# Retention, queries and keys of batches 1 to 3 worked inside the attention of the batch before, through one PSUM bank

## The reference, cut to what matters

```python
sq, sk, sv = (_lin(x, Wsq, bsq), _lin(x, Wsk, bsk), _lin(x, Wsv, bsv))   # 16 heads of 8
g = jnp.exp(-jax.nn.softplus(_lin(x, Wg, bg)))                          # one gate a head
def step(M, inp):                                                       # over the 1024 tokens
    g_t, k_t, v_t, q_t = inp
    M = g_t[..., None, None] * M + k_t[..., None] * v_t[..., None, :]
    h = jnp.einsum('bhd,bhde->bhe', q_t, M)
    return (M, h)
Q, K = _l2norm(_lin(Hseq, Wq, bq)), _l2norm(_lin(Hseq, Wk, bk)); V = _lin(x, Wv, bv)
scores = jnp.einsum('bhqd,bhkd->bhqk', Q, K) * jax.nn.softplus(temp)
out = jnp.einsum('bhqk,bhkd->bhqd', jax.nn.softmax(scores, axis=-1), V)
return _lin(out, Wo, bo)
```

## Time and profile before

| | |
|---|---|
| median of 3 runs | 1385.3 us (1382.85 to 1386.9) |
| the profiled execution | 1391.36 us, of which its span 1389.4 us |
| PE busy | 1071.3 us, 77% of the span |
| ACT busy | 975.3 us, 70% |
| DVE busy | 742.7 us, 53% |
| POOL busy | 325.7 us, 23% |
| constants, up to the first DMA of the first layer norm | 0 to 4.75 us of the span |
| retention, all batches | 504.6 to 669.6 us |
| queries and keys, all batches | 669.6 to 735.1 us |
| attention | 735.1 to 1220.0 us |

### The profile page before, as it was taken

The page is one execution under the profiler, slowest core; times in us unless marked ns, Lnnn a source line. Parts: engine busy times, 40 slices in busy tenths (PEclk is TensorE's granted clock), DMA queues, the critical chain, the costliest instruction groups (busy, mean ns, idle before and its releaser), DMA issues. The chain is left out here.

```text
span 1389.4 us, 17492 instructions
## 1 busy us (share of the span) xinstructions
PE 1071.3 (77%) x5850; PEld 393.9 (28%) x5850; DVE 742.7 (53%) x1012; ACT 975.3 (70%) x884; POOL 325.7 (23%) x194
## 2 busy tenths in 40 slices
PE   4748777777799956777446888888888888679996
PEld 3213333333344422332341111111111111134443
DVE  5869998987566648998481001200300300256664
ACT  3767665754688832221336999999999999658885
POOL 3117776766111114665100000000000000011110
PEclk8769999999899978998777999999999999879998
DMA  2000100100100000000001111111111111000002
GB/s 73 0 16 30 31 30 30 60 30 31 32 30 30 31 24 0 0 0 1 8 0 33 24 24 32 37 24 28 22 33 34 24 24 28 11 31 31 30 30 61
DMA packets 24188, 36.48 MB, mean 26 GB/s; under 512 B 7362, under 2 KB 11970, under 8 KB 24130
## 3 DMA queue, kind: packets, MB, share of 16 engines
q1 hardware_dynamic: 24130, 35.71, 9.5%
HBM read 16.82 MB, written 6.29 MB: 17 GB/s over the span
## 5 line engine op out<-in xcount | busy, mean ns | idle before, releaser
L1674 ACT ACTIVATE att_prob<-att_s_ps 128x1536 f32<-128x1536 f32 x342 | 459.2, 1912 | 7.4 <-PE att_s_ps L1588 7.3
L1603 PE MATMUL att_o_ps<-att_prob,att_va 128*32 128x512 f32 x2048 | 273.9, 607 | 0.5 <-ACT att_prob L1674 0.5
L1705 DVE COPY att_o_sb<-att_o_ps 128x512 f32<-128x512 f32 x32 | 22.1, 691 | 381.7 <-PE att_o_ps L1603 381.7
L1588 PE MATMUL att_s_ps<-att_q_st,att_k_st 32*128 32x512 f16 x1024 | 134.4, 388 | 80.8 <-ACT att_prob L1674 76.1
L685 POOL TENSOR_TENSOR scan_hc<-scan_state,scan_c_rep 128x1024 f32<-128x1024 f32 x64 | 151.9, 2392 | 71.9 <-DVE scan_state L642 71.7
L787 POOL TENSOR_TENSOR ffn_veps<-ffn_mv,all_eps 128x4 f32<-128x4 f32 x16 | 9.1, 570 | 575.3 <-DVE ffn_mv L944 575.3
L642 DVE TENSOR_TENSOR_SCAN scan_state<-scan_decay,scan_drive_ps 128x1024 f32<-128x1024 f32 x64 | 142.9, 2270 | 0.3 <-ACT scan_decay L615 0.3
L282 PE MATMUL scan_y_ps<-scan_hc,all_ident 128*128 128x512 f32 x256 | 130.2, 634 | 8.3 <-DVE scan_y_sb L661 6.2
L1588 PEld LDWEIGHTS att_s_ps<-att_q_st,att_k_st 32*128 32x128 f16 x1024 | 33.1, 91 | 327.2 <-ACT att_prob L1674 315.9
L619 ACT ACTIVATE scan_c_rep<-scan_c_ps 128x1024 f32<-128x1024 f32 x64 | 65.4, 1022 | 80.4 <-PE scan_c_ps L282 80.1
L1012 DVE SCALAR_TENSOR_TENSOR ffn_hid_lo<-ffn_hid,ffn_share,ffn_hid_hi 128x1024 f16<-128x1024 f32 x64 | 81.9, 1283 | 48.8 <-ACT ffn_hid_hi L920 48.1
(11 more groups left out here) (215 smaller groups left out, 1505.8 us busy)
## 6 DMA issues: line engine op xcount, KB each, us to landing
...
att_q_st<-hv_part SPq DMA_DIRECT2D x64, 64.0 KB, 2.1
att_k_st<-hv_part SPq DMA_DIRECT2D x64, 64.0 KB, 2.1
...
```

The lines of the kernel that those rows point to most:

```text
L1588: last = pe.matmul(s_ps[e % 2][:, n, :], k_st[rows, g % 2, kc * P:(kc + 1) * P], q_st[rows, g % 2, HALVES[half]], start=True, stop=True)
L1603: last = pe.matmul(o_ps[half][32 * j:32 * j + 32, :], va[:, g % 2, kc, j, :], prob[:, (GH * v + j) % RING, :], start=kc == 0, stop=kc == K ...
L1674: act.activation(prob[:, first % RING:first % RING + n, :], s_ps[e % 2][:, 0:n, :], ACT.Exp).then_inc(exped.sem, 1)
```

## The change

Retention and queries-and-keys run as stages of their own for batch 0 only. For batches 1 to 3 the same results are made by pieces of work, called guests here, that all engines do between their attention instructions of the batch before, at step `u = v % 64`. All guest products go through one PSUM bank of 512 columns, `b_ps`, in halves of 512 tokens. To free that bank, the two score buffers become a triple and a pair, so that Exp instructions take 1536 and 1024 columns in turn. The guest gate is Exp on ACT (table of Exp stays loaded), then +1 and a reciprocal on DVE. Copies that ACT did (splits, keys, queries, values, h) go to DVE, squares to POOL; the root stays on ACT. Guest products write `kv_sb` in SBUF instead of multiplying in PSUM, so the guest scan reads gate and input from SBUF. SP's `stack` of a batch's first head group waits for the last of the guest's splits. `v_tok` and `part` hold two batches in turn.

Besides: the retention weights, `wo`, softplus(temp), the output bias and `a_neg` are loaded or worked out in `load_constants`; the staging copies `dt_b` and `h_b` are gone; all `Fori` loops outside the first layer norm and the store are written out; at the end of each stage POOL clears the stage's semaphores; the splitting of the expert weights in `selective_scan` takes every seventh step; `divide` is spread over steps 5, 7, 9, 11 and the projection is at steps 12 and 14 (before: all at step 5, and 11 and 13).

The diff, cut to its core:

```diff
 def load_constants(t, whole):
+                sp.dma_start(w_all[:, 0:len(RET_MATS), :], d["ret_mats"]).then_inc(ret_loaded, 16)
+                sp.dma_start(w_all[:, len(RET_MATS):W, :], d["wsv"]).then_inc(ret_loaded, 16)
+                ... (head_sum, att_mats, bqk, wo: four more DMAs; SP waits for all)
+                act.activation(t.ret_hi[:, :, :], w_all[:, :, :], ACT.Copy, scale=WS).then_inc(ret_high, 1)
+                dve.scalar_tensor_tensor(t.ret_lo[:, :, :], w_all[:, :, :], WS, t.ret_hi[:, :, :], ALU.mult,
+                                         ALU.subtract)
 def attention(t):
-    WIDE, BEHIND, RING = (2, 3, 12) if following else (3, 2, 15)
+    WIDE, CYCLE, BEHIND, RING = (3, 2), 5, 2, 15
-    DIVIDE_AT, PROJECT_AT = W + 5, (W + 11, W + 13)
+    DIVIDE_AT, PROJECT_AT = (5, 7, 9, 11), (12, 14)
+    TURN_X_AT, NORMAL_AT, TURN_Z_AT = (0, 6), (2, 8), (4, 10)
+    MAKE_AT = 11
+    OPEN_AT, INVERT_AT = (16, 19), ((17, 18), (22, 25))
+    SUM_AT = (34, 45)
+    PROJECT_QK_AT = (37, 40, 47, 48)
+    REDUCE_AT = (39, 42, 49, 50)
+    ROOT_AT, RECIPROCAL_AT, UNIT_AT, TURN_QK_AT = 53, 54, (55, 55, 56, 56), (56, 57, 58, 59)
+    def closes(e):
+        return (tiles_of(e)[-1] + 1) // GH > tiles_of(e)[0] // GH
+    def unit_at(u):
+        return [w for w in range(UNITS) if 20 + 3 * w // 2 == u]
 # PE, after scores(e) and the values that are due, where a group closes step v:
+                def make(n, p):
+                    elif x == 2:
+                        pe.wait_ge(gated.sem, gated.at(n - 1, h))
+                        last = parts(b_ps[:, :], t.ret_hi[:, w, :], t.ret_lo[:, w, :], z_hi[:, HALVES[h]], z_lo[:, HALVES[h]])
+                def key_value(n, w):
+                        pe.wait_ge(kv_done.sem, kv_done.at(n - 1, w - 1))
+                    parts(b_ps[:, :], t.ret_hi[:, i, :], t.ret_lo[:, i, :], z_hi[:, HALVES[h]],
+                          z_lo[:, HALVES[h]]).then_inc(v_made.sem, 1)
+                def add_heads(n, h):
+                    for odd in range(2):
+                        for c in range(4):
+                            last = pe.matmul(b_ps[32 * c:32 * c + 32, :], t.head_sum[:, odd, :], qm[:, 4 * odd + c, :],
+                                             start=not odd, stop=bool(odd))
 # ACT
+                def gate(n, h):
+                    act.wait_ge(made.sem, made.at(n - 1, 4 * h + 1))
+                    act.activation(g_sb[:, HALVES[h]], b_ps[:, :], ACT.Exp, bias=t.col("bg"),
+                                   scale=1.0 / WS).then_inc(gated.sem, 1)
+                def root(n):
+                    act.wait_ge(clipped.sem, clipped.at(n - 1))
+                    act.activation(rn[:, :, :], ss[:, :, :], ACT.Sqrt).then_inc(rooted.sem, 1)
                 for e in range(GROUPS):
                     ... (the Exp of group e)
+                    if closes(e):
+                        n, u = guest(first // GH)
+                        if u in (MAKE_AT + 2, MAKE_AT + 6):
+                            gate(n, (u - MAKE_AT) // 4)
+                        if u == ROOT_AT:
+                            root(n)
 # DVE
+                def invert_gate(n, h, k):
+                    dve.reciprocal(g_sb[:, cols], g_sb[:, cols]).then_inc(gate_made.sem, 1)      # 256 columns
+                def outer(n, w):
+                    dve.scalar_tensor_tensor(kv_sb[:, w % 2, :], b_ps[:, :], t.bsv_large[:, m:m + 1], k_sb[:, HALVES[h]],
+                                             ALU.add, ALU.mult).then_inc(kv_done.sem, 1)
+                def scan(n, w):
+                    dve.tensor_tensor_scan(mem[:, m, :], g_sb[:, HALVES[h]], kv_sb[:, w % 2, :],
+                                           mem[:, m, HALF - 1:HALF] if h else 0.0, ALU.mult,
+                                           ALU.add).then_inc(scanned.sem, 1)
 # POOL
+                def weigh(n, w):
+                    pool.tensor_tensor(qm[:, m, :], mem[:, m, :], q_sb[:, HALVES[h]], ALU.mult).then_inc(weighed.sem, 1)
 # SP
                 def stack(g):
+                    if g % G == 0 and g:
+                        sp.wait_ge(lo_done.sem, lo_done.at(g // G - 1, 3))
 def hybrid_layer(nc, dram):
-            retention(t)
-            queries_and_keys(t, s)
-            attention(t, list(range(B)), [])
+            retention(t, batches[:1])
+            queries_and_keys(t, batches[:1])
+            attention(t)
```

880 lines of the change are left out of this document (500 added, 380 removed).

## The result

The kernel after takes 1351.1 us (median of 4 runs, 1345.3 to 1352.2) where the kernel before took 1386.1 beside it: ratio 0.9745, 95% interval 0.9728 to 0.9762. It is faster, by 35 us; the forecast was 1303, with a range of 1270 to 1345. The profiled execution took 1350.3, its span 1348.5; the sum had said 1308.7. So the sum was 41.6 us short.

The account below looks back on a forecast made before the run. Attention was taken as bound by ACT, with PE's small room overrun by guests. Removed stages -148.3, constants +0.6, Exp +4.0, guests +57, projection +4.0 make -82.7: 1391.4 to 1308.7 profiled, median 1303, range 1270 to 1345.

Parts of the forecast that it names:

- the bunches' reserve: Guest batches in attention: four bunches of guests start with ACT fed ahead, which saves 0.4 us for each.
- What was removed, and the weights: Stages before attention: three batches leave, -148.3 us; loads and splits moved to the constants: -2.4, -4.2 and +7.2, net +0.6.
- the written-out loops: Loops written out, semaphores cleared and `dt_b` gone: 0 us, bounds -8 and +3, as no row showed a price.
- Exp in triples and pairs: ACT in attention: 410 Exp groups, 68 more, at 0.06 us each, +4.0 us; upper bound +11.4.
- The projection: Projection with `wo` at steps 12 and 14, beside makes, no longer fits PE's room: +4.0 us, bounds 0 and 4.5.
- The guests: Guest batches in attention: work beyond PE's room and stalls at gates, root and stack, 19 us a batch, 57 for three.
- PE's prices: PE in attention: a unit or make occupies 0.65 us, room is 0.36 a step; guests 27.8 a batch against 23.0.
- DVE as the bound of steps 20 to 33, with POOL excluded: Attention: DVE needs 34.5 us against 30.8 from step 17, 5 of it POOL and scans excluding each other; 3.5 taken.
- The root's tables: ACT at step 53: two table loads of 1.28 us each and 0.4 for 256 columns, 3.0 us a batch.
- Rival 2: Attention: round trips of `b_ps` between PE and DVE rule, 35 us a batch, median 1355; chance 0.21.
- Rival 3: Attention: stalls bring PE's clock down to the 1.2 GHz level, median above 1385, so slower; chance 0.04.
- Rival 1: Attention: PE absorbs the guests, only 8 to 9 us a batch left, median 1268; chance 0.15.

Follow-up runs that it names:

- e15_best: Also called the best run. Against the kernel after: values one group later, gate one step earlier, root as Newton steps on DVE, earlier turns; 1289.9 us, ratio 0.9302.

## Why the prediction was wrong

Excess of guest batches 1, 2, 3 by step (the forecast's projection, 0, 2, 2, stands in steps 10 to 19):

| steps | forecast | after | e15_best |
|---|---|---|---|
| 0 to 9 | 0 | 2.0, 0.9, 1.4 | 2.2, 0.5, 0.7 |
| 10 to 19, makes, gates, projection | 6, 8, 8 | 10.5, 11.9, 11.3 | 3.9, 6.0, 5.9 |
| 20 to 33, ten units | 3.5 | 5.1, 5.5, 4.7 | 3.6, 3.3, 3.8 |
| 34 to 43, units, head sum, two projections | 4.6 | 8.6, 7.7, 8.1 | 5.8, 5.9, 5.0 |
| 44 to 48 | 2.5 | 2.9, 2.8, 2.7 | 2.6, 2.5, 2.7 |
| 49 to 54, root | 3.0 | 3.1, 3.2, 3.6 | 0.7, 0.4, 0.2 |
| 55 to 62, turns | 0 | 4.4, 5.1, 5.6 | 1.2, 1.6, 1.3 |
| 63, stack | 1.0 | 0.9, 2.8, 1.3 | 0.1, 0, 0 |
| sum | 20.6, 22.6, 22.6 (19, 21, 21 less the bunches' reserve) | 37.6, 39.8, 38.6 | 20.1, 20.2, 19.6 |

**What was removed, and the weights:** right. 154.9 forecast, 156.0 measured from retention's first copy to the first Exp. The constants end at 11.28 in place of 4.75, +6.5 for +7.2. Yet retention starts 2.0 earlier, not 7 later: from the end of the constants to its first copy it is 491.8 us for 500.3, where the forecast had put the written-out loops at 0 without a row. In all 18 traces of kernels with the new code there this stretch takes 487 to 496, but the kernel before has one trace, of its slowest execution, so how much the loops brought stays open.

**Exp in triples and pairs:** right. 51.2 x 2.26 = 115.7 a batch for 85.3 x 1.343 = 114.6 is +4.4 in all, forecast +4.0.

**The projection:** right. In the best run steps 10 to 16 have 3.6, 5.1 and 5.4 in batches 1 to 3, the latter two with a projection: 1.5 and 1.8 more than batch 1, 3.3 for the 4.0 forecast. The last batch has 1.4 there, with a projection and no guests, where the forecast had none.

**The guests:** the step that failed. "I take 19, nearer to the sums of occupied time than to a wait at each guest, as most guests have a step of 1.8 us for a DVE operation of 0.7." They measured some 37 (37.6 in batch 1, which has no projection beside it), so this one term accounts for nearly all of the 55 us by which the excess of three batches, 116.0, is over the forecast's 61. An average step was taken for the distance between guests. Where every step has a guest, two of five in PE's order follow the one before after 0.32 us, and PE, with the next scores behind it, stands until DVE's 0.74 are over. By the runs, attention loses, with one thing taken away at a time: the hand-overs between adjacent guests 22.7, the gates 10.9, with ACT's own 6 x 0.7 still there (forecast 6 x 1.7 = 10.2 for both; a gate was 2.7), the root's tables 7.7 (forecast) and what follows them 5.7 (PE at half clock), which was not in the sum. The earlier chain with the stack gave 13.9 on the kernel with guests later, whose stack had been put back by a group. Together the best run takes away 56.0, and its guest batches have an excess of 20.0, where the forecast had 21 with the projection. In that run the forecast of "near 135" is met (135.7); but its root costs nothing, where 3.0 were counted, so the agreement hides some 3 us a batch that other terms had too little.

**PE's prices:** units 0.75 for 0.65, room 0.30 for 0.36. For ten units over 14 steps this gives 7.5 - 4.2 = 3.3, against 3.6, 3.3, 3.8 in the best run; the 5.8, 5.9, 5.0 of steps 34 to 43 stand over the forecast's 4.6 for the same reason. An estimate from these two prices, 0.1 for each of 22 products and 0.06 for each of 36 steps with guests, is 4.4 a batch, 13 of the gap. That PE's occupied time still sets the length where guests are products is shown by the cut of its work, 19.3 us.

**DVE as the bound of steps 20 to 33, with POOL excluded:** wrong as a mechanism. The forecast's 3.5 is near the best run's 3.6, by chance: cutting scans and POOL's products by three quarters changes 0.0 there. What POOL costs a scan is in the trace, and small: a scan that started beside POOL took 1.76 in place of 1.28 (at 681.20 in the trace after), while POOL's product kept its 1.28. Only 11 of 48 scans are longer than 1.4, which makes some 1.5 us a batch where the forecast had 5. That POOL contends with DVE instructions of two inputs in SBUF is what the Trainium skill states (GPSIMD Engine Reference, Specifications and Key points), and the trace agrees. The rest of the step's sum was right: the forecast had DVE at work for 29.5 us from step 17 to 33, and in the windows view of the best run it is busy for 28.5 of these steps' 35.0 (761.5 to 796.5). PE is busy for 34.1 of them, and so what DVE does is hidden.

**The root's tables:** the row's 1.28 was right; from the end of one Exp to the next it is 3.03 with two loads (1020.03 to 1023.06). The 2.7 a load of the Trainium skill (ScalarE: Activation LUTs, What ACT_TABLE_LOAD costs) would have put them 5.8 apart, and the trace does not show it.

**The rivals.** Rival 2, the single bank's round trips, gave 1355, nearly the measured time, but by chance: it had them as a rule for every guest and from steps 17 to 33, where DVE was to be late. Measured is a part of it, at adjacent guests, not only from step 17 to 33, 22.7 of 116 us; the rest of the gap is other things. Rival 3, the clock, is there in small: 31 us at half clock, not the whole of attention; the mean over attention is 0.97. Rival 1 did not come.
